# A new head, a new order at the boundary, and the first expert tile's silu without its table, in a two-layer kernel on one core

## The reference

```
x = norm(x + rwkv(x))          # k, v, r = (x*m + shifted x*(1-m)) @ W ; scan over time ; sigmoid(r) * out ; @ Wo
x = norm(x + moe(x))           # 8 experts, top 2 of the router's logits, softmax of the two;
                               # silu(x @ gate[e]) * (x @ up[e]) @ down[e], width 176
x = norm(x + linear_attn(x))   # 16 heads, elu + 1
x = norm(x + bitlinear_ffn(x)) # ternary weights, width 704, sigmoid gate
```

## Time and profile before

| | us |
|---|---|
| median of three runs (400.18, 400.77, 407.91) | 400.77 |
| the profiled execution | 400.25 |
| its span, first to last instruction | 398.4 |
| mean granted TensorE clock | 0.975 |

### The profile page before, as it was taken

How to read it: one execution, slowest core, us unless ns; L and a number is a source line. 1 busy time by engine, 2 the same in 40 slices (tenths; PEclk the granted TensorE clock), 3 DMA queues, 4 the chain that set the end, 5 groups by cost and what they waited for, 6 DMA issues and landing times.

```text
span 398.4 us, 7791 instructions
## 1 busy us (share of the span) xinstructions
PE 361.3 (91%) x2440; PEld 323.8 (81%) x2440; DVE 292.1 (73%) x748; ACT 210.5 (53%) x483; POOL 137.4 (34%) x233
## 2 busy tenths in 40 slices
PE   8999999999598999999999847999999999999790
PEld 8999889998476877767777736999999999999680
DVE  6996999999974584895453264797879788876741
ACT  6664677668555333355335414556555564646451
POOL 4001077776717520030310268244536240311201
PEclk9999999999789999999999998999999999999986
DMA  7899411111234357533521131102021100000000
GB/s 224 299 307 243 145 55 41 40 55 54 75 99 133 120 176 247 147 105 101 153 81 53 54 92 54 53 2 81 10 73 33 48 29 0 28 2 26 0 28 26
DMA packets 28567, 35.79 MB, mean 90 GB/s; under 512 B 3696, under 2 KB 25712, under 8 KB 28272
## 3 DMA queue, kind: packets, MB, share of 16 engines
q1 hardware_dynamic: 19696, 21.78, 18.4%
q0 software_dynamic: 3072, 8.39, 6.6%
q10 hardware_dynamic: 5760, 5.12, 3.9%
HBM read 22.83 MB, written 12.45 MB: 89 GB/s over the span
## 4 chain that ended last, share of the span: by engine, by line
PE 49%; DVE 34%; issue 8%; ACT 4%; POOL 3%; DMA 1%; ACTq 0%; DVEq 0%; POOLq 0%
PE bank L414 19%; PE bank L558 10%; PE bank L579 8%; DVE st L1110 4%; PE bank L750 2%; PE bank L424 2%; PE bank L695 2%; PE bank L538 2%; PE bank L568 2%; DVE arena L1599 2%; DVE arena L1592 2%; DVE arena L1173 2%; DVE arena L1197 1%; DVE arena L1494 1%; ACT arena L1073 1%
## 5 line engine op out<-in xcount | busy, mean ns | idle before, releaser
L812 ACT ACTIVATE arena<-bank 128x256 f32<-128x256 f32 (+1 forms) x118 | 45.3, 422 | 40.1 <-PE bank L579 28.9
L1688 POOL TENSOR_TENSOR ve<-mv,eps 128x2 f32<-128x2 f32 x32 | 8.1, 252 | 158.8 <-DVE mv L1114 111.5
L558 PE MATMUL bank<-gu,arena 128*128 x156 | 52.6, 460 | 0.0
L817 ACT ACTIVATE arena<-arena,nm,rs 128x256 f32<-128x256 f32 x48 | 26.2, 596 | 39.8 <-POOL nm L1696 39.6
L1772 POOL DMA_INDIRECT arena<-yg,ypos x32 | 31.2, 974 | 38.9 <-DMA yg<-arena 30.4
L579 PE MATMUL bank<-dn,arena 96*128 x156 | 41.1, 385 | 2.4 <-DVE arena L1370 2.4
L1370 DVE COPY arena<-bank 96x256 f32<-96x256 f32 x39 | 16.3, 419 | 33.3 <-PE bank L568 32.9
L1742 POOL DMA_INDIRECT xg<-x,pos x32 | 35.4, 1107 | 14.3 <-issue 7.3
L579 PEld LDWEIGHTS bank<-dn,arena 96*128 96x128 f32 x156 | 28.6, 190 | 11.9 <-issue 4.3
L414 PE MATMUL bank<-arena 128*128 128x256 f32 (+2 forms) x192 | 34.3, 321 | 3.4 <-DVE arena L1185 1.9
L414 PE MATMUL bank<-x_hi,w1q 128*128 128x256 f32 x128 | 36.0, 305 | 1.5 <-ACT x_hi L812 1.5
(11 more groups left out here) (275 smaller groups left out, 1120.0 us busy)
## 6 DMA issues: line engine op xcount, KB each, us to landing
arena<-xg SPq DMA_DIRECT2D x39, 128.0 KB, 2.1
yg<-arena ACTq DMA_DIRECT2D x39, 128.0 KB, 1.7
arena<-in_xT SPq DMA_DIRECT2D x8, 256.0 KB, 5.9
x<-in_x SPq DMA_DIRECT2D x8, 256.0 KB, 4.5
out<-arena SPq DMA_DIRECT2D x8, 256.0 KB, 2.1
gu<-in_w_gate SPq DMA_DIRECT2D x1, 1408.0 KB, 9.7
gu<-in_w_up SPq DMA_DIRECT2D x1, 1408.0 KB, 13.8
dn<-in_w_down SPq DMA_DIRECT2D x11, 128.0 KB, 6.5
```

Of the source, the lines that this page charges most:

```text
L558: last = pe.matmul(bank[BANK_GU[i % 2]][:, 0:2 * F], xtT[:, i % 2, chunk(k)], w[:, :, k, :, bass.ds(e, 1), :], start=k == 0, stop=k == KC - 1)
L812: return act.activation(dst, src, ACT.Copy)
L817: last = act.activation(dst[:, t, :], src[:, t, :], ACT.Identity, bias=nm[:, i, t:t + 1], scale=rs[:, i, t:t + 1])
```

## The change

**Head.** PE warms up with 11 matmuls in place of 16. The first k projection is issued in the order in which its operands become ready (`first_keys`), the same 24 products. ACT and DVE split x of block 0 after the first half of the first weight, and x of block 1 only after the first k (ACT) and the first `exponents` (DVE).

**Slots.** Projections may be issued by half (12 matmuls). `output(now)` now stands ahead of the v projection in slots 0 and 1, and between its halves after that. `rank` stands between the halves of the r projection.

**Routing weights.** POOL's and ACT's routing weights per block (three POOL operations and two ACT operations) go; one difference, one tanh and two POOL operations over all tokens are made during the expert phase, ACT's part at tile 12.

**Boundary.** In slot 6 DVE puts `choose(4)`, `positions(4)` and `first_places` between the scans. After slot 6 the table of the first tiles is finished before `differences(7)`. ACT normalises block 5 ahead of the last exponentials and copies tile 0's turned rows between the gate's two operations. PE turns block 5 ahead of `output(6)`, and `output(7)` stands behind `turn_hidden(0)` and `gate_up(2)`.

**First silu.** Tile 0 gets 1/(1+exp(-g)) by relu, exp, ln and exp (`sigmoid`), ahead of the last `reciprocal` and of the table load, and one more DVE multiply by g.

**Pads.** SP writes four of the eight pads. ACT writes the other four, one each behind `store(5)`, `store(6)`, `store(7)` and `store(8)`.

```diff
@@ PE, a slot
-                if 0 <= new < B:
+                value_bank = halves(1 + new % 2)
+                if new == 0:
+                    first_keys(halves(0))
+                else:
                     past(pe, ku_ok, new)
-                    project(new, 0, halves(0), kp_mm)
-                if 0 <= old < B:
-                    turn_x1(old)
-                if 0 <= new < B:
-                    past(pe, cv_ok, new - 1)
-                    project(new, 1, halves(1 + new % 2), vp_mm)
-                if 0 <= old < B:
+                    project(new, 0, halves(0), kp_mm, (0,))
+                    if old == FULL_AT - 1:
+                        turn_x1(old)
+                    project(new, 0, halves(0), kp_mm, (1,))
+                past(pe, cv_ok, new - 1)
+                if old == FULL_AT - 1:
                     logits(old)
-                if 0 <= now < B - 1:
-                    output(now)
-                if old == FULL_AT - 1:
+                    project(new, 1, value_bank, vp_mm, (0,))
                     rank(old)
                     first_total()
-                if 0 <= new < B:
-                    past(pe, gate_ok, new)
-                    project(new, 2, halves(3), rp_mm)
+                elif 0 <= old:
+                    turn_x1(old)
+                    project(new, 1, value_bank, vp_mm, (0,))
+                    logits(old)
+                if 0 <= now:
+                    output(now)
+                project(new, 1, value_bank, vp_mm, range(1 if 0 <= old else 0, KC))
+                if old == FULL_AT - 1:
+                    tile_order(0, bank[7][:, 4 * E:4 * E + 1])
+                past(pe, gate_ok, new)
+                project(new, 2, halves(3), rp_mm, (0,))
                 if 0 <= old < FULL_AT - 1:
                     rank(old)
+                project(new, 2, halves(3), rp_mm, (1,))
@@ PE, the first tiles
+            turn_x1(B - 3)
             output(B - 2)
-            turn_x1(B - 3)
+            turn(0)
             for i in range(3):
                 experts[i] = expert_of(i)
-            turn(0)
-            logits(B - 3)
             turn(1)
             gate_up(0, experts[0])
+            logits(B - 3)
             turn(2)
             gate_up(1, experts[1])
+            turn(3)
+            tile_front(0)
             rank(B - 3)
             output(B - 1)
-            turn(3)
-            tile(0)
+            tile_back(0)
@@ ACT
+            def pad(e):
+                if e == E // 2:
+                    act.wait_ge(zero_ok, 1)
+                    act.wait_ge(pads_ok, 1)
+                r0 = act.value_load(table[0:1, T_PAD + e:T_PAD + e + 1], min_val=e * REGION, max_val=e * REGION + NTOK)
+                act.dma_start(xg[bass.ds(r0, P), :], zero[:, :]).then_inc(pad2_ok, 16)
+            def sigmoid(i):
+                act.wait_ge(gu_ok, i + 1)
+                stepped(act.activation(sg[:, i % 2, :], bank[BANK_GU[i % 2]][:, 0:F], ACT.Relu, bias=floor[:, :]))
+                stepped(act.activation(sg[:, i % 2, :], sg[:, i % 2, :], ACT.Exp, bias=floor[:, :], scale=-1.0))
+                stepped(act.activation(sg[:, i % 2, :], sg[:, i % 2, :], ACT.Ln, bias=1.0))
+                act.activation(sg[:, i % 2, :], sg[:, i % 2, :], ACT.Exp, scale=-1.0).then_inc(sg_ok, 1)
...
+                if 5 <= i < 5 + E // 2:
+                    pad(i - 5 + E // 2)
+                if i == 12:
+                    odds()
@@ SP
-            for e in range(E):
+            for e in range(E // 2):
...
-            sp.wait_ge(pad_ok, 16 * E)
+            sp.wait_ge(pad_ok, 16 * (E // 2))
+            sp.wait_ge(pad2_ok, 16 * (E // 2))
@@ DVE, slot and boundary
+                if old == FULL_AT - 1:
+                    weighted_values(s)
                     choose(old)
-                if 0 <= now:
-                    residual(now)
-                if old == FULL_AT - 1:
+                    weights_state(s)
                     positions(old)
...
                     first_places()
+                    values_state(s)
...
+            outputs(B - 1)
+            hidden(0)
+            choose(B - 3)
+            hidden_turned(0)
...
             finish_y(B - 1)
             residual(B - 2)
-            hidden(0)
             positions(B - 3)
-            hidden_turned(0)
+            spread(B - 2)
             hidden(1)
             residual(B - 1)
+            spread(B - 1)
```

More of the change, by code:

```diff
@@ L46 @@
 FULL_AT = 5
-GATED = B - 3
 ROOT = 16
@@ L144, in build @@
         sel = sb("sel", [P, NTILE, 2])
-        gap = sb("gap", [P, NT])
+        gap = sb("gap", [P, NTILE])
         topw = sb("topw", [P, NTILE, 2])
@@ L425, in transposes, with project @@
                 return last
-            def project(b, j, dst, done):
-                if j == 0:
+            def project(b, j, dst, done, parts=range(KC)):
+                if j == 0 and 0 in parts:
                     pe.wait_ge(xsl_ok, b + 1)
                 if b == 0:
-                    pe.wait_ge(wlow_ok, j + 1)
-                for d in range(KC):
+                    pe.wait_ge(wlow_ok, j + 2)
+                for d in parts:
                     last = product(dst[:, d, :], [
@@ L436, in project, with first_keys, add @@
                                           [s[b % 2][:, k, 1 - lag:1 - lag + T] for s in (xs_hi, xs_lo)])])
-                last.then_inc(done, 1)
+                if KC - 1 in parts:
+                    last.then_inc(done, 1)
+            def first_keys(dst):
+                def add(w, x, k, first=False, final=False):
+                    for lag in range(2):
+                        for d in range(KC):
+                            last = pe.matmul(dst[:, d, :], w[0][:, lag * KC + k, chunk(d)],
+                                             x[0][:, k, 1 - lag:1 - lag + T],
+                                             start=first and lag == 0 and d == 0, stop=final and lag == 1,
+                                             skip_group_check=True)
+                    return last
+                pe.wait_ge(xsh_ok, 1)
+                pe.wait_ge(whigh_ok, 2)
+                add(wA_hi, xs_hi, 0, first=True)
+                pe.wait_ge(wlow_ok, 1)
+                add(wA_lo, xs_hi, 0)
+                pe.wait_ge(whigh_ok, 4)
+                add(wA_hi, xs_hi, 1)
+                pe.wait_ge(xsl_ok, 1)
+                add(wA_hi, xs_lo, 0)
+                add(wA_hi, xs_lo, 1)
+                pe.wait_ge(wlow_ok, 2)
+                add(wA_lo, xs_hi, 1, final=True).then_inc(kp_mm, 1)
             def output(b):
@@ L884, in gate_exponentials, with odds @@
                 stepped(act.activation(gate[:, :, :], halves(3), ACT.Relu, bias=floor[:, :]))
+                if s == B - 1:
+                    turned(0)
                 act.activation(gate[:, :, :], gate[:, :, :], ACT.Exp, bias=floor[:, :], scale=-1.0).then_inc(gate_ok, 1)
-            def odds(b):
-                act.wait_ge(route_step, 4 * b + 1)
-                past(act, topw_ok, 3 * b)
-                for t in range(NT):
-                    last = act.activation(gap[:, t:t + 1], mx8[:, t, 0:1], ACT.Exp, bias=mx8[:, t, 1:2], scale=-1.0)
-                last.then_inc(odds_ok, 1)
-            def gaps(b):
-                act.wait_ge(gap_ok, b - GATED + 1)
+            def odds():
+                act.wait_ge(gap_ok, 1)
                 act.activation(gap[:, :], gap[:, :], ACT.Tanh, scale=0.5).then_inc(odds_ok, 1)
@@ L1336, in a_slot @@
                     first_places()
+                    values_state(s)
+                else:
+                    states(s)
+                    if 0 <= old:
+                        choose(old)
+                if 0 <= now:
+                    residual(now)
                 outputs(s)
@@ L1739, in scatter @@
                 pool.wait_ge(pos_ok, b + 1)
-                for n in range(NT * b, NT * (b + 1)):
+                for n in (NT * b + t for t in parts):
                     for j in range(2):
```

159 lines of the change are left out of this document (77 added, 82 removed).

## The result

The changed kernel took 405.63 us (median of 4 runs, 405.39 to 407.27) against 401.22 for the kernel before beside it; the ratio is 1.0132, 95% interval 1.0098 to 1.0167. One of the executions of the kernel before (407.91 us) fell in a slower state and is left out of the ratio. So the change costs 1.3%: 4.4 us between the medians, 5.3 by the ratio. My number was 401.5, with 397.0 to 405.5 as its range. The change is within 2%, as forecast, but the loss is over three times the 1.2 us of my sum, and the time lies just above the range.

A forecast was written before the change was run, and what follows sets the result against it. No engine bounds the whole: DVE paces the slots with PE close behind, PE the tiles. Against the profiled 400.25 us, -3.2 (head) + 1.4 (boundary) + 3.0 (pads) = +1.2 gave 401.5 us, range 397.0 to 405.5.

The forecast's parts named there:

- Head, -3.2: Start of the kernel: earlier v projection and `output(0)` ahead of it remove DVE's idle time before the first residual, -3.2 us.
- The slots: Slots: DVE sets the pace, routing weights lie beside its work and half projections keep their count, so 0 us.
- Boundary, +1.4: From slots to tiles: block 6's normalisation and turning come later behind the new silu and `hidden(0)`, +1.4 us.
- Pads, +3.0: Expert tiles: ACT's last pad stands behind `store(8)`, so PE waits for tile 13's rows, +3.0 us.
- The clock falls in the 3 us wait at tile 13: Rival at tile 13: half of a low-clock stretch falls on running tiles, +3 us, 404.5 us in all; chance 0.10.
- the pads were not in time: Rival at tile 13: the pads are there in time and the +3.0 us falls away, 398.5 us; chance 0.15.
- the head gave more than 1.3: Rival in the head: only PE's 1.3 us come, another wait replacing the one for `output(0)`, 403.4 us; chance 0.06.
- PE did not come to pace the slots: Rival in the slots: PE sets the pace, 1.45 us held up per slot, 8.7 over six, 410.2 us; chance 0.04.
- the first rival: Rival at the boundary: the clock stays at 2.4 GHz over `output(6)`, gaining 1.9 us and 0.6 behind it, 399.0 us; chance 0.15.

The follow-up runs named there:

- experiment 4: Changed kernel, but in slots 0 and 1 PE does the whole v projection ahead of `output(0)` again: 408.53 us, ratio 1.0234 to the kernel before.
- experiment 2: Changed kernel with PE's `output(6)` ahead of block 5's turning, and ACT's normalisation of block 5 behind its exponents of block 7: 407.48 us, ratio 1.0186.
- experiment 3: Changed kernel with tile 0's silu from the table again and the old order behind `gate_up(1)` on PE, ACT and DVE: 405.03 us, ratio 1.0116.
- experiment 7: Changed kernel with the last `reciprocal` ahead of the exponential silu, `finish_y(7)` and `output(7)` ahead of tile 0's hidden rows: 406.17 us, ratio 1.0118.
- experiment 10: Changed kernel with last `reciprocal` ahead of the exponential silu, `finish_y(7)` and `output(7)` ahead of tile 0's hidden rows, block 6's normalisation ahead of `evacuate(0)`: 406.41 us.
- experiment 5: Changed kernel with 26 unused matmuls of a constant on PE between `down(9)` and the turning of tile 13: 406.48 us, ratio 1.0115.
- experiment 11: Head and routing weights alone, rest put back or mended, plus 15 unused matmuls ahead of `output(6)` and 6 ahead of block 7's turning: 396.87 us, ratio 0.9919.
- experiment 12: Changed kernel plus unused matmuls on PE: 15 ahead of block 5's turning, 6 ahead of block 7's, 13 ahead of tile 13's: 401.03 us, ratio 1.0012.
- experiment 1: Changed kernel with all eight pads issued by SP again: 401.08 us, ratio 1.0015 to the kernel before.
- experiment 6: Changed kernel with ACT's four pads all issued in a row behind tile 5: 403.14 us, ratio 1.0047 to the kernel before.
- experiment 8: Changed kernel keeping only head and routing weights; pads, tile 0's silu and `output(6)` order put back, ACT's copy behind gate exponentials: 398.55 us, ratio 0.9926.

## Why the prediction failed

**Head, -3.2: right**, measured -3.5, and for the reason given: the order took the idle time away (experiment 4: 2.1 of it), the earlier start gave the rest. The slots cost nothing, as said.

**Boundary, +1.4: this step failed in size**, it was +3.3. The chain was the right one, link by link: the last `reciprocal` behind the silu, `finish_y(7)` behind `hidden(0)`, block 6's normalisation and turning late, `down(0)` not early. The 1.9 us that were missing lie in two places. With the head's measured 3.5 us off, my sum has `gate_up(0)` at 108.5, and it came at 109.52: 1.0 late. There the sum put block 5's turning ahead of `output(6)` at nothing, as work that falls into idle time, and left `output(6)` at 106.65, that is 103.1 now. It began at 104.60, since the turning waited for ACT's normalisation, which waited for POOL. The sum had given POOL's scatters in front of that a start 2 us earlier; POOL was ready at 102.52, which is 106.0 in the times of the trace before, against 106.65 there: only 0.6 earlier. `output(6)` and what follows it up to `gate_up(0)` then took 4.9 us and not 5.35, though `turn(1)` waited 0.63 us in it for ACT's copy of tile 0's rows. The other 0.9 lie behind: from `gate_up(0)` to the turning of block 6 I had 10.35 us and it took 11.24. The silu was done 3.1 us behind the start of `gate_up(0)` and not 2.65 (gate and up took 1.43 and not 1.2, the four operations 1.64 and not 1.45), and `evacuate(0)`, a row of ACT's queue that the sum did not name, held the normalisation 0.4 us longer.

**Pads, +3.0: right**, measured +3.2, with the last pad, the load and the turning in the order and nearly the distances given.

**The clock: this step failed most.** "The clock falls in the 3 us wait at tile 13" stood among the rivals with a chance of 0.10 and +3; it happened, at 2.3. The sum had this term at nothing. In the profiled kernels with that wait left empty it fell every time (six of six: the changed kernel and experiments 2, 3, 4, 7 and 10), and in the eight without it, or with it filled, never. The trace before had shown the same thing at 105.0: a wait, then half the clock on the work behind it. I had used that row for the boundary, and then counted the wait which I myself put at tile 13 at its bare length. The Trainium skill ("TensorE: Matmul & The Clock Gate", What's actually happening) has the gate follow how busy PE has recently been; by that alone the rival's +3 belonged in the sum. The traces agree: the clock fell in the wait left empty and not in the filled one.

Put together, -3.5 + 3.3 + 3.2 + 2.3 = +5.3 on 400.25 gives 405.55, the measured median within 0.1. That closeness is partly luck. The terms are read off one execution of each kernel, and the changed one has 1.5 us at block 7 on top, which I had nowhere. That fall is not in every execution: behind the same 1.75 us of idle time it came in four profiled kernels (the changed one, 3, 5 and 10) and stayed away in eight, the kernel before among them; with that wait filled, in experiments 11 and 12, it stayed away too. Whether the three shorter executions of the changed kernel are the ones without it is not shown: their mean granted clock, 0.962 to 0.963, is no higher than the profiled one's 0.963. Nor is the stretch at the boundary fixed: it lasted some 4 us in experiments 1, 3, 6 and 8, and 7 or more in the other kernels without a fill there.

**The other rivals.** The clock did not stay up at `output(6)`, the pads were not in time, the head gave more than 1.3, and PE did not come to pace the slots. The point that PE has too little work there (the ground against the first rival) was right; only filling the wait with matmuls changed it.

Not settled: how often each low stretch comes in executions that were not profiled, and what sets the length of the one near 235 us. With it goes where four of six executions lost again what the 13 matmuls at tile 13 had saved.

## What to carry to other kernels

A wait that a change gives to PE can cost more than its length, as the one at tile 13 did (3.2 us and 2.3 of low clock): read what the clock did behind the nearest wait of the same length, and price the work behind the new one at that. When a short operation is moved ahead of another chain, walk the queue of every engine on that chain and name each row that now stands in front, the copies and evacuations too; a step moved on one engine alone moves the wait. Before you put a step into another's idle time, look when its own input is ready. And take a gain apart at one event of the trace at a time: here a head that won 3.5 us was hidden behind three later losses.

## What the runs showed of the hardware

- **Work that nobody needs can pay.** 15, 6 and 13 matmuls of a constant by itself (each two instructions of 0.115 us) in PE's waits took 4.6 us off the changed kernel (405.63 to 401.03, ratios 1.0132 and 1.0012).
- **Short idle time is enough for the clock at times.** It fell behind 1.75 us in four profiled executions of twelve, and in two it fell in the slots: at 42 us in experiment 4, and at 53 in experiment 6. In the 2 us from 50 to 52 PE was busy 1.46 us there and 1.50 in the changed kernel, whose clock stayed up: nearly the same work went both ways.
- **A start of a transfer holds its engine for long where its address is first loaded from a table.** Four pads in a row kept ACT from its work for 4.78 us, though the starts themselves are rows of 0.35 each. Behind a store, whose address is fixed, ACT stood 0.19 us (last two rows).

```profile
141.71 3.52 ACTq L1013 DMA_DIRECT2D xg<-zero  x4
145.34 0.32 ACT L976 ACTIVATE arena<-bank 128x176 f32<-128x176 f32 x1 [4.78 <-issue]
...
145.96 0.34 ACTq L985 DMA_DIRECT2D yg<-arena  x1
146.40 0.32 ACT L976 ACTIVATE arena<-bank 128x176 f32<-128x176 f32 x1 [0.19 <-issue]
```
